# The entry of a two-layer transformer kernel: group 0's padded queries and keys from padded weights, later norms on ACT

## The chip, the cores and the metric

The kernel runs on one core of one Trainium2 chip. The metric is the device time of one execution in microseconds (us). The core has the matrix engine PE (its weight loads are listed apart as PEld), the vector engine DVE, the scalar engine ACT, GpSimd (POOL), and SyncE (SP), which here issues nearly all DMA transfers. The engines run apart from one another and meet at semaphores. Each takes its own instructions strictly in order, so an instruction that waits holds back everything behind it on its engine.

## The reference

Input is x, 4 sequences of 512 tokens of width 128 (2048 tokens). Four sublayers follow, each as `x = x + f(layernorm(x))`:

```
Q, K, V = heads(x @ WQ), heads(x @ WK), heads(x @ WV)      # 16 heads of width 8
score = Q K^T / sqrt(8) + causal mask; softmax; out = P V; out @ WO
mixture of 8 experts, top 2, capacity limit, GELU
gated linear recurrence (16 heads of 64) and an FFN, itself a pre-norm block
FFN of ternary weights: silu(xW1)*(xW2), two GELU layers, W3
```

Only the entry matters here: the first layernorm, `Q` and `K` of sequence 0, and the first score tiles of the first attention.

## The kernel before, in words

**Work units.** Attention goes by batch (sequence) b = 0..3 and by group g = 0..3 of four heads; w (or G) = 4b + g numbers the 16 groups. For each group PE computes ten row tiles of 128 queries by 4 heads x 128 keys (`row_scores`, fp32r, into one of three PSUM banks that rotate, `ROWB = 3`), and DVE takes the maximum of each (`row_max`). `minus_max` forms the negated maxima, PE turns them (`turn_max`), DVE adds them into the queries (`add_max`, QM), and then the second pass begins: `key_scores` on PE, exp on ACT, a causal select on POOL, `values` on PE. The row tiles of group w+1 run between the second-pass tiles of group w. A group takes about 10 us in steady state.

**Padded operands.** A head is only 8 wide. To keep fp32 accuracy in fp32r, Q and K are split into a rounded high part and a low rest, and each head takes 32 partitions: for the queries the planes high, low, high, 0; for the keys high, high, low, 1. The fourth plane later carries the maximum. In the kernel before, every group gets these padded tiles through DRAM: `project(b)` (two fp32 matmuls, L1537 and L1538) writes Q and K, ACT rounds them (`round_halves`, L659), DVE subtracts to get the low part (`make_halves`, L977), SP stores six planes into `qk_dram` (`store_planes`), and `pad(G)` reads back QS (queries, one DMA, L398) and KP (keys, four DMAs, one per head, block-diagonal over zeros that POOL has set, L407).

**The entry.** SP loads x by batch. DVE makes the statistics of batch 0 (L960 to L967), POOL the reciprocal root (a power, L494), DVE the norm (L947, `first_norm`). PE turns the normed tile (`first_turn`, L1516), ACT copies it out (`keep_x`, L645), PE projects. The statistics of batches 1 to 3 are one stretch of twelve tiles on DVE. Their norms come on DVE behind `make_halves(0)`. For each batch PE then does a turn and the values' projection (`first_v`, L1525), and ACT copies both out (`keep_x`, `keep_v`). Only when all four batches are done does PE start `row_scores(0, 0)`. Behind the ten tiles of group 0 stand a wait for the last `keep_v`, the first two row tiles of group 1, and `turn_max(0)`.

**What sets the order.** Nothing is scheduled by a planner: each engine's program is written out by hand in its order, and PSUM banks are handed over by counters (`rs_full`, `row_free`). `RING` numbers the uses of the three row banks: the Q and K projections of batch 0 take places 0 and 1 (banks 0 and 1), group 0's tiles the places from 2 on.

Of the kernel before, what the change touches and what calls it, by code (L numbers as in the profile page):

```python
# [13 lines left out]
P = 128  # L14
NB = 4
# [26 lines left out]
N_CONST = 3 * P + 16 + 2 * NT + 8  # L42
# [66 lines left out]
def build(nc, d):  # L109
    ctx = ExitStack()  # L110
    with ctx:
# [3 lines left out]
        def sem(name):  # L115
            return ctx.enter_context(nc.semaphore(name))
# [15 lines left out]
        iota8 = const[:, 3 * P + 16 + 2 * NT:3 * P + 24 + 2 * NT]  # L132

# [116 lines left out]

        ones = low["h2_w"][:, FF - 1, :].bitcast(F32)
# [34 lines left out]
        var0, rs0, xn0, tp0, tc0, vp0, vc0 = (sem(n) for n in ("var0", "rs0", "xn0", "tp0", "tc0", "vp0", "vc0"))  # L286
        l0 = sem("l0")
# [63 lines left out]
        def _(sp):  # L351
# [38 lines left out]
            def pad(G):  # L390

                b, g = G // NG, G % NG
                if g == 0:
                    sp.wait_ge(pads_out[b], 32)
                    sp.wait_ge(q_planes, 48 * (b + 1))
# [4 lines left out]
                if g == 0:  # L400
                    sp.wait_ge(k_planes, 48 * (b + 1))
# [8 lines left out]
            pad(0)  # L410
# [71 lines left out]
        def _(g):  # L482
# [12 lines left out]

            first_rsqrt(0, slice(0, TB))
            set_keys(0)
            first_rsqrt(1, slice(TB, NT))
            set_keys(1)
# [132 lines left out]
        def _(act):  # L632
# [262 lines left out]
        def _(v):  # L895
# [610 lines left out]
        def _(pe):  # L1506
            pe.wait_ge(par_in, 32)
# [145 lines left out]
            for u in range(10):
                row_scores(0, u)
# [385 lines left out]
def shape_constants():  # L2040
# [17 lines left out]
    c[:, at:at + 8] = np.arange(8)  # L2058

# [33 lines left out]
```

## Time and profile before

| | us |
|---|---|
| median of 3 runs | 664.29 (663.62 to 668.38) |
| profiled execution, its own time | 664.96 |
| its span | 663.2 |
| granted TensorE clock, mean over the span | 0.963 |
| PE busy | 579.7 (87%) |
| DVE busy | 406.9 (61%) |
| ACT busy | 308.9 (47%) |
| POOL busy | 172.6 (26%) |

A span runs from the first to the last profiled instruction; the execution's own time has 1.8 us more around it. Busy shares are averages over the whole program, and the change touches only its first few dozen microseconds, so what counts is the order of time there: which instruction is released by which.

### The profile page before, as it was taken

To read this page: it belongs to the slowest core of one execution; us is meant where nothing else is said; L and a number is where in the kernel's file an instruction comes from. 1 tells how busy PE (TensorE), PEld (TensorE's weight loads), DVE (VectorE), ACT (ScalarE), POOL (GpSimd) and SP (SyncE) were. 2 spreads that over 40 slices of the span, in tenths; PEclk is the share of its full clock that TensorE was granted. 3 is DMA by queue.
4 is the path that set the end of the run, shared out by engine and by line. 5 is a ranking of instruction groups with operands and counts; after the bars stand their busy time and mean duration, and the time that the engine had idled before them with its cause. 6 is when DMAs were issued, how large, how long until landed. Compare 5 with 4: busy or idle time off the path is not lost.

```text
span 663.2 us, 9219 instructions
## 1 busy us (share of the span) xinstructions
PE 579.7 (87%) x3331; PEld 433.6 (65%) x3331; DVE 406.9 (61%) x959; ACT 308.9 (47%) x527; POOL 172.6 (26%) x184
## 2 busy tenths in 40 slices
PE   2689999999999559999828698899999999998987
PEld 1546656556665346877726486688778878786866
DVE  5678868978886421332237985994569656762330
ACT  3336665555656213453305343852565355653351
POOL 4302212352452640000057643601400041001100
PEclk9999999999999759999959897999999999999999
DMA  4746241262210425753111000000000000000000
GB/s 133 220 128 217 96 138 35 64 192 64 72 57 1 123 77 194 236 177 113 32 51 27 22 16 1 25 9 1 0 17 1 0 1 17 1 0 1 16 1 17
DMA packets 45645, 43.02 MB, mean 65 GB/s; under 512 B 4256, under 2 KB 34976, under 8 KB 45600
## 3 DMA queue, kind: packets, MB, share of 16 engines
q1 hardware_dynamic: 43264, 37.96, 18.9%
q0 software_dynamic: 2048, 4.20, 2.1%
q8 instruction: 27, 0.44, 0.3%
q10 hardware_dynamic: 288, 0.27, 0.2%
q14 instruction: 18, 0.15, 0.1%
HBM read 25.64 MB, written 16.78 MB: 64 GB/s over the span
## 4 chain that ended last, share of the span: by engine, by line
PE 70%; DVE 11%; issue 7%; ACT 7%; DMA 2%; POOL 2%; SPq 1%; DVEq 0%; ACTq 0%; POOLq 0%
PE ps L1865 7%; PE ps L1818 6%; PE ps L1547 6%; PE ps L1809 5%; PE ps L1563 5%; PE ps L1575 5%; PE ps L1887 5%; PE ps L1888 4%; PE ps L1968 4%; PE ps L1964 4%; PE ps L1965 4%; PE ps L1891 4%; DVE pm L987 2%; PE ps L1881 2%; PE ps L1550 2%
## 5 line engine op out<-in xcount | busy, mean ns | idle before, releaser
L669 ACT ACTIVATE PT<-ps 128x384 f32<-128x384 f32 (+1 forms) x192 | 93.4, 529 | 75.2 <-PE ps L1563 69.6
L987 DVE TENSOR_REDUCE pm<-ps 128x4 f32<-128x512 f32 x160 | 102.0, 684 | 11.7 <-PE ps L1547 11.3
L1547 PE MATMUL ps<-KP,QS 128*128 128x512 f32 x160 | 72.2, 453 | 6.1 <-DVEq L980 3.2
L536 POOL TENSOR_SCALAR_AFFINE_SELECT PT<-PT 128x512 f32<-128x512 f32 x64 | 39.9, 636 | 133.9 <-ACT PT L669 133.1
L1563 PE MATMUL ps<-QM,KP 128*128 128x512 f32 (+3 forms) x256 | 69.2, 331 | 1.6 <-DVE QM L1001 1.1
L1563 PEld LDWEIGHTS ps<-QM,KP 128*128 128x128 f32 x256 | 43.7, 189 | 23.0 <-issue 13.4
L757 ACT ACTIVATE HT<-ps,cols 128x640 f32<-128x640 f32 x32 | 25.4, 793 | 54.9 <-PE ps L1809 54.9
L1547 PEld LDWEIGHTS ps<-KP,QS 128*128 128x128 f32 x160 | 29.9, 188 | 27.2 <-DVE pm L987 13.5
L1352 DVE TENSOR_TENSOR_SCAN zero<-decay,OG 128x512 f32<-128x512 f32 x32 | 44.8, 1401 | 1.1
L1575 PE MATMUL ps<-PT,V 128*32 128x128 f32 (+3 forms) x512 | 44.6, 442 | 0.0
L511 POOL TENSOR_TENSOR rstd<-veps,mhalf 128x4 f32<-128x4 f32 x11 | 12.7, 1157 | 111.4 <-DVE veps L924 111.2
L1818 PE MATMUL ps<-W,HT 128*128 128x128 f32 x320 | 37.9, 278 | 3.1 <-ACT HT L757 3.1
L1818 PEld LDWEIGHTS ps<-W,HT 128*128 128x128 f32 x320 | 36.3, 192 | 5.3 <-ACT HT L757 5.3
L1809 PE MATMUL ps<-XST,W 128*128 128x320 f32 x128 | 36.5, 438 | 1.1 <-DVE XST L1253 1.1
L814 ACT ACTIVATE hF<-ps,cols 128x512 f32<-128x512 f32 x16 | 11.0, 687 | 56.1 <-PE ps L1968 56.1
L1347 DVE SCALAR_TENSOR_TENSOR OG<-ps,cols,vs 128x512 f32<-128x512 f32 x32 | 24.0, 749 | 18.1 <-ACT vs L793 14.2
L797 ACT ACTIVATE gs<-ps,half_bg 128x512 f32<-128x512 f32 x32 | 22.0, 688 | 26.7 <-PE ps L1891 25.6
L601 POOL DMA_INDIRECT G<-ys_dram,posG x8 | 7.6, 950 | 93.1 <-DMA ys_dram<-zero 91.0
L572 POOL DMA_INDIRECT G<-ys_dram,posG x24 | 29.3, 1221 | 6.8 <-issue 6.8
L793 ACT ACTIVATE vs<-ps,cols 128x512 f32<-128x512 f32 x32 | 22.0, 687 | 19.2 <-PE ps L1891 19.1
L1809 PEld LDWEIGHTS ps<-XST,W 128*128 128x128 f32 x128 | 22.4, 190 | 12.1 <-ACT HT L757 4.4
L1865 PEld LDWEIGHTS ps<-lwo,oT 128*128 128x128 f32 x256 | 29.1, 192 | 0.2
(279 smaller groups left out, 1303.1 us busy)
## 6 DMA issues: line engine op xcount, KB each, us to landing
qk_dram<-HL SPq DMA_DIRECT2D x24, 256.0 KB
QS<-qk_dram SPq DMA_DIRECT2D x16, 256.0 KB
KP<-qk_dram SPq DMA_DIRECT2D x64, 64.0 KB
W<-in_eW SPq DMA_DIRECT2D x16, 256.0 KB
xs_dram<-zero SPq DMA_DIRECT2D x4, 640.0 KB, 3.7
XS<-xs_dram SPq DMA_DIRECT2D x8, 320.0 KB, 4.6
ys_dram<-zero SPq DMA_DIRECT2D x8, 320.0 KB, 2.9
whole_h_w<-in_h_w SPq DMA_DIRECT2D x2, 1024.0 KB, 9.1
```

The lines of the kernel that those rows point to most:

```text
L536: g.affine_select(out=diag, in_=diag, pattern=[[0, 4], [1, P]], compare_op=ALU.is_ge, fill=0.0, base=0, channel_multiplier=-1).then_inc(se ...
L572: g.indirect_dma_start(out=G[:, b % 2, i, :], out_offset=None, in_=ys_dram, in_offset=bass.IndirectOffsetOnAxis(ap=posG[:, c:c + 1], axis= ...
L669: act.activation(PT[:, i, a:z], bank[ROWB + n % KEYB][:, 0:z - a], ACT.Exp, scale=float(DK) ** -0.5).then_inc(exp_done, 1)
L987: v.tensor_reduce(pm[:, t, k, :], bank[n % ROWB].rearrange("p (i n) -> p i n", n=P), AXX, ALU.max).then_inc(row_free[n % ROWB], 1)
L1352: v.tensor_tensor_scan(st, decay[:, f:f + 1].to_broadcast([P, SEQ]), kv, 0.0, ALU.mult, ALU.add).then_inc(st_done, 1)
L1547: mm = pe.matmul(to, QS[:, G % 2, t * P:(t + 1) * P], KP[:, G % 3, k, :, :].rearrange("p i n -> p (i n)"), start=True, stop=t != k)
L1563: mm = pe.matmul(bank[ROWB + n % KEYB][:, at:at + SEQ - j * P], KP[:, w % 3, j, i, :], QM[:, w % 2, j * P:SEQ], start=True, stop=True)
L1575: mm = pe.matmul(bank[6][32 * i:32 * i + 32, j * P:SEQ], V[:, j * H + g * 4 + i, :], PT[:, i, OFF[j]:OFF[j + 1]], start=(j == 0), stop=(j ...
L1809: mm = pe.matmul(ps[:, 2 * (f % 2) + a, 0:HALF], W1[:, s, f * P:(f + 1) * P], XST[:, s, a * HALF:(a + 1) * HALF], start=True, stop=True)
L1818: mm = pe.matmul(bank[4 + j // 4][:, (j % 4) * P:(j % 4 + 1) * P], HT[:, s, f, j * P:(j + 1) * P], W2[:, s, f, :], start=(f == 0), stop=(f ...
L1865: mm = pe.matmul(bank[5][:, t * P:(t + 1) * P], src[:, f, t * P:(t + 1) * P], w[:, f, :], start=(f == 0 and t == 0), stop=(f == n - 1), sk ...
L1887: pe.matmul(to, high[n][:, cs], halves_of[:, 0, :], start=True, stop=False)
```

## The change

Group 0's padded tiles are no longer read back from DRAM. DVE clears two 128x128 tiles (in a part of VR that is not in use yet) and copies columns of WK and WQ into them, four heads at 32 columns each, with the sign of the plane (for the keys w, w, -w, 0; for the queries w, -w, w, 0). Two fp32 matmuls with these weights (into banks 3 and 7) give the padded keys and queries at once. ACT writes the rounded value, and one DVE instruction adds or subtracts the exact value with a per-partition factor 0 or -1 (three new columns of `const`), so that each plane becomes its high or low part. The padded queries land in QS directly. The keys are spread into their diagonal blocks by two DVE and two ACT copies of 32 partitions. Groups 1 to 3 of batch 0 still come through DRAM, so the plain projections, the halves and the stores stay; `pad(1)` is now the first load.

The norms of batches 1 to 3 move from DVE to ACT, as x * rstd + (-mean * rstd). DVE makes -mean, POOL the product. POOL's two first clears of KP move ahead of its first power, DVE's clears of MX and pm move to its very start. PE gets six matmuls on a tile of zeros before anything else, and the ten row tiles of group 0 stand between the turns and value projections of batches 1 to 3. `ROWB` stays 3.

PE, from its start to the first `turn_max` (L1516 first_turn, L1525 first_v, L1547 and L1550 row_scores and its mask, L1589 turn_max), before:

```order
L1516 MATMUL ps<-const,xn 128x128 x4
L1537 MATMUL ps<-xnT,wq 128x512
L1538 MATMUL ps<-xnT,wk 128x512
L1516 MATMUL ps<-const,O 128x128 x4
L1525 MATMUL ps<-wv,xnT 128x128 x4
L1516 MATMUL ps<-const,xn 128x128 x4
L1525 MATMUL ps<-wv,xnT 128x128 x4
L1516 MATMUL ps<-const,O 128x128 x4
L1525 MATMUL ps<-wv,xnT 128x128 x8
L1547 MATMUL ps<-KP,QS 128x512 x2
```

And the same place in the changed kernel (L1711 and L1713 are the padded keys and queries, L1581 first_turn, L1590 first_v, L1615 and L1618 row_scores):

```order
L1571 MATMUL ps<-zero 128x512 x6
L1581 MATMUL ps<-const,xn 128x128 x4
L1711 MATMUL ps<-xnT,VR 128x512
L1713 MATMUL ps<-xnT,VR 128x512
L1602 MATMUL ps<-xnT,wq 128x512
L1603 MATMUL ps<-xnT,wk 128x512
L1590 MATMUL ps<-wv,xnT 128x128 x4
L1615 MATMUL ps<-KP,QS 128x512 x2
L1618 MATMUL ps<-mask,identr 128x512
L1615 MATMUL ps<-KP,QS 128x512 x2
L1581 MATMUL ps<-const,O 128x128 x4
L1615 MATMUL ps<-KP,QS 128x512
```

The row tiles now start behind batch 0's value projection, and batch 1's turn stands behind four of them; the two padded projections stand ahead of the plain ones.

ACT, from batch 0's turned tile (L655 keep_x) to its last copy of values (L659 keep_v) in the changed kernel (L715 and L717 round the padded tiles, L709 spreads keys, L669 rounds the plain halves, L704 is the norm):

```order
L655 ACTIVATE xnT<-ps 128x512
L715 ACTIVATE low_Wv<-ps,const 128x512
L717 ACTIVATE QS<-ps 128x512
L709 ACTIVATE KP<-low_Wv 32x4x128 x2
L669 ACTIVATE HL<-ps 128x512 x2
L659 ACTIVATE VR<-ps 128x512
L704 ACTIVATE O<-X,VR,rstd 128x128 x4
L655 ACTIVATE xnT<-ps 128x512
L704 ACTIVATE xn<-X,VR,rstd 128x128 x4
L659 ACTIVATE VR<-ps 128x512
L655 ACTIVATE xnT<-ps 128x512
L704 ACTIVATE O<-X,VR,rstd 128x128 x4
```

Before, ACT had only the L645, L649 and L659 copies here; the twelve norm instructions are new, and so are the four on padded tiles, which stand ahead of the halves that the stores wait for.

POOL, its first instructions in the changed kernel (L492 clears KP, L502 the powers, L509 the product, L510 clears V):

```order
L496 MEMSET low_h_w 128x512
L492 MEMSET KP 128x2048 x2
L502 ISA
L502 TENSOR_TENSOR rstd<-veps,mhalf 128x4
L502 TENSOR_TENSOR rstd<-veps,mhalf 128x12
L509 TENSOR_TENSOR VR<-VR,rstd 128x12
L510 MEMSET V 128x2048
```

Before, the row marked ISA (a setting that POOL takes ahead of its first power) stood right behind the clear of low_h_w, and each power had a clear of KP behind it.

The diff, with comments and the parts that only repeat left out:

```diff
@@ -132 +133 @@
+low_q, low_k, pad_k = (const[:, N_CONST - 3 + i:N_CONST - 2 + i] for i in range(3))
@@ -250 +252 @@
+wqp = VR[:, NT - 1, :]
+wkp = VR[:, NT - 2, :]
+first_k = low["Wv"][:, 0:SEQ]
+nm0 = VR[:, NT - 3, 0:NT]
+nmr0 = VR[:, NT - 3, NT:2 * NT]
@@ -393 +402 @@
-        if g == 0:
+        if g == 0 or G == 1:
@@ -400 +409 @@
-        if g == 0:
+        if g == 0 or G == 1:
@@ -410 +418 @@
-    pad(0)
@@ -496 +503 @@
-    first_rsqrt(0, slice(0, TB))
@@ -498 +504 @@
-    first_rsqrt(1, slice(TB, NT))
@@ -499 +506 @@
+    first_rsqrt(0, slice(0, TB))
+    first_rsqrt(1, slice(TB, NT))
+    g.wait_ge(rs0, 2)
+    g.tensor_tensor(nmr0[:, TB:NT], nm0[:, TB:NT], rstd0[:, TB:NT], ALU.mult).then_inc(rs0, 1)
@@ -688 +699 @@
+    def first_norm(b):
+        dst = (xn, O)[b % 2]
+        if b >= 2:
+            act.wait_ge(tp0, b - 1)
+        for t in range(b * TB, (b + 1) * TB):
+            ins = act.activation(dst[:, t % TB, :], X[:, t, :], ACT.Identity, scale=rstd0[:, t:t + 1],
+                                 bias=nmr0[:, t:t + 1])
+        ins.then_inc(xn0, 1)
+    def spread_keys(i):
+        act.activation(KP[32 * i:32 * i + 32, 0, :, i, :],
+                       first_k[32 * i:32 * i + 32, :].bitcast(F32).rearrange("p (t n) -> p t n", n=P),
+                       ACT.Copy).then_inc(first_a_set, 1)
@@ -689 +714 @@
+    act.wait_ge(first_full, 1)
+    act.activation(first_k, bank[3], ACT.Identity, bias=pad_k).then_inc(first_high, 1)
+    act.wait_ge(first_full, 2)
+    act.activation(QS[:, 0, :], bank[7], ACT.Identity).then_inc(first_high, 1)
+    act.wait_ge(first_sum, 1)
+    act.wait_ge(kp_set, 1)
+    spread_keys(2)
+    spread_keys(3)
@@ -691 +723 @@
-    for b in range(1, NB):
-        keep_x(b)
-        keep_v(b - 1)
-    keep_v(NB - 1)
+    keep_v(0)
+    act.wait_ge(rs0, 3)
+    first_norm(1)
+    keep_x(1)
+    first_norm(2)
+    keep_v(1)
+    keep_x(2)
+    first_norm(3)
+    keep_v(2)
+    keep_x(3)
+    keep_v(3)
@@ -940 +979 @@
-    def first_norm(b):
-        dst = (xn, O)[b % 2]
-        v.wait_ge(rs0, min(b, 1) + 1)
-        if b >= 2:
+    v.memset(wqp, 0.0).then_inc(wp_zero, 1)
+    v.memset(wkp, 0.0).then_inc(wp_zero, 1)
+    v.memset(MX[:, :, :, :].bitcast(F32), 0.0)
+    v.memset(pm[:, :, :, :], -3.0e38)
@@ -945 +984 @@
-            v.wait_ge(tp0, b - 1)
-        for t in range(b * TB, (b + 1) * TB):
-            ins = v.tensor_scalar(dst[:, t % TB, :], X[:, t, :], mv0[:, t, 0:1], rstd0[:, t:t + 1],
-                                  ALU.subtract, ALU.mult)
-        ins.then_inc(xn0, 1)
-    for ts in (range(0, TB), range(TB, NT)):
-        if ts[0]:
-            first_norm(0)
-            v.memset(MX[:, :, :, :].bitcast(F32), 0.0)
-            v.memset(pm[:, :, :, :], -3.0e38)
+    def first_stats(ts):
@@ -966 +996 @@
+        if ts[0]:
+            v.tensor_scalar(nm0[:, c], mv0[:, c, 0], -1.0, None, ALU.mult)
@@ -968 +1000 @@
+    def planes(w):
+        return w.rearrange("p (h c r) -> p h c r", h=4, c=4)
+    def of_heads(w, n):
+        return w[:, 0:4 * DK].rearrange("p (h a r) -> p h a r", h=4, a=1).to_broadcast([P, 4, n, DK])
+    first_stats(range(0, TB))
+    v.wait_ge(wqk_in, 32)
+    v.wait_ge(wp_zero, 2)
+    v.tensor_copy(planes(wkp)[:, :, 0:2, :], of_heads(wk, 2))
+    v.tensor_scalar(planes(wkp)[:, :, 2:3, :], of_heads(wk, 1), -1.0, None, ALU.mult).then_inc(wp_set, 1)
+    v.tensor_copy(planes(wqp)[:, :, 0:3:2, :], of_heads(wq, 2))
+    v.tensor_scalar(planes(wqp)[:, :, 1:2, :], of_heads(wq, 1), -1.0, None, ALU.mult).then_inc(wp_set, 1)
+    v.wait_ge(rs0, 1)
+    for t in range(TB):
+        ins = v.tensor_scalar(xn[:, t, :], X[:, t, :], mv0[:, t, 0:1], rstd0[:, t:t + 1], ALU.subtract, ALU.mult)
+    ins.then_inc(xn0, 1)
+    first_stats(range(TB, NT))
+    def add_low(n, dst, src, sign, done):
+        v.wait_ge(par_in, 32)
+        v.wait_ge(first_high, n)
+        v.scalar_tensor_tensor(out=dst, in0=src, scalar=sign, in1=dst.bitcast(F32), op0=ALU.mult,
+                               op1=ALU.add).then_inc(done, 1)
+    add_low(1, first_k, bank[3], low_k, first_sum)
+    v.wait_ge(first_sum, 1)
+    v.wait_ge(kp_set, 1)
+    for i in (0, 1):
+        v.tensor_copy(KP[32 * i:32 * i + 32, 0, :, i, :],
+                      first_k[32 * i:32 * i + 32, :].bitcast(F32).rearrange("p (t n) -> p t n", n=P)
+                      ).then_inc(first_v_set, 1)
+    add_low(2, QS[:, 0, :], bank[7], low_q, first_v_set)
@@ -1090 +1154 @@
-    first_norm(1)
-    first_norm(2)
-    first_norm(3)
@@ -1506 +1569 @@
+    pe.wait_ge(zero_set, 1)
+    for _ in range(6):
+        pe.matmul(bank[7], zero[:, 0:P], zero[:, 0:SEQ], start=True, stop=True)
@@ -1543 +1608 @@
-        if u == 0:
-            pe.wait_ge(qs_in[G % 2], 16 * (G // 2 + 1))
-            pe.wait_ge(kp_in[G % 3], 64 * (G // 3 + 1))
+        if u == 0 and G == 0:
+            pe.wait_ge(first_v_set, 3)
+            pe.wait_ge(first_a_set, 2)
+        elif u == 0:
+            pe.wait_ge(qs_in[G % 2], 16 * ((G + 1) // 2))
+            pe.wait_ge(kp_in[G % 3], 64 * ((G + 2) // 3))
@@ -1641 +1710 @@
+    pe.wait_ge(wp_set, 1)
+    pe.matmul(bank[3], wkp, xnT[:, 0:SEQ], start=True, stop=True).then_inc(first_full, 1)
+    pe.wait_ge(wp_set, 2)
+    pe.matmul(bank[7], wqp, xnT[:, 0:SEQ], start=True, stop=True).then_inc(first_full, 1)
@@ -1644 +1715 @@
-    first_turn(1)
@@ -1647 +1718 @@
-    first_turn(2)
+    pe.wait_ge(bfc, 4)
+    row_scores(0, 0)
+    row_scores(0, 1)
+    row_scores(0, 2)
+    row_scores(0, 3)
+    first_turn(1)
+    row_scores(0, 4)
+    row_scores(0, 5)
@@ -1649 +1727 @@
-    first_turn(3)
+    first_turn(2)
+    row_scores(0, 6)
+    row_scores(0, 7)
@@ -1650 +1731 @@
+    first_turn(3)
+    row_scores(0, 8)
+    row_scores(0, 9)
@@ -1652 +1734 @@
-    pe.wait_ge(bfc, 4)
-    for u in range(10):
-        row_scores(0, u)
@@ -2058 +2139 @@
+    at += 8
+    plane = i % 32 // 8
+    c[:, at] = np.where(plane == 1, -1.0, 0.0)
+    c[:, at + 1] = np.where(plane == 2, -1.0, 0.0)
+    c[:, at + 2] = plane == 3
```

## Rows read from the trace of the kernel before

**Rows 1.** The chain in order of time, 0 to 110 us: start, length, what.

```profile
17.77 4.68 DVE O L947 x3
22.49 1.11 PE ps L1516 x4
...
30.14 6.08 DVE pm L987 x10
...
37.79 0.69 DVE QM L1001
```

**Rows 2.** Timeline, DVE, 4 to 49 us: start, length, line, instruction, xcount, idle before.

```profile
7.93 2.37 DVE L947 TENSOR_SCALAR xn<-X,mv,rstd 128x128 f32<-128x128 f32 x4 [1.20 <-POOL rstd L494]
...
10.84 2.35 DVE L960 BATCH_NORM_STATS2 stats<-X 128x6 f32<-128x128 f32 x12
...
14.27 0.17 DVE L967 TENSOR_SCALAR veps<-mv 128x12 f32<-128x12 f32 x1
...
17.51 4.93 DVE L947 TENSOR_SCALAR O<-X,mv,rstd 128x128 f32<-128x128 f32 x4 [0.15 <-DVE HL L977]
22.36 1.10 DVE L947 TENSOR_SCALAR xn<-X,mv,rstd 128x128 f32<-128x128 f32 x4
```

**Rows 3.** Timeline, PE, 10 to 50 us.

```profile
10.45 1.08 PE L1516 MATMUL ps<-const,xn 128*128 128x128 f32 x4 [10.45 <-DVE xn L947]
...
14.09 1.91 PE L1538 MATMUL ps<-xnT,wk 128*128 128x512 f32 x2
...
27.37 0.60 PE L1516 MATMUL ps<-const,O 128*128 128x128 f32 x4
...
42.72 1.12 PE L1537 MATMUL ps<-xnT,wq 128*128 128x512 f32 x2
...
46.26 0.45 PE L1547 MATMUL ps<-KP,QS 128*128 128x512 f32 x1
...
48.31 0.50 PE L1547 MATMUL ps<-KP,QS 128*128 128x512 f32 x1 [1.21 <-DVEq L980]
```

**Rows 4.** Timeline, ACT, 4 to 31 us.

```profile
5.30 0.31 ACT L636 ACTIVATE identr<-const 128x128 fp32r<-128x128 f32 x1 [2.22 <-DMA cols<-in_cols]
...
30.40 0.62 ACT L696 ACTIVATE V<-VR 128x512 f32<-128x512 f32 x1
```

**Rows 5.** Timeline, POOL, 0 to 40 us.

```profile
1.93 0.53 POOL L488 MEMSET low_h_w<- 128x512 f32 x1
6.88 1.01 POOL L494 TENSOR_TENSOR rstd<-veps,mhalf 128x4 f32<-128x4 f32 x1 [4.42 <-DVE veps L967]
7.84 1.81 POOL L484 MEMSET KP<- 128x2048 f32 x1
14.53 2.28 POOL L494 TENSOR_TENSOR rstd<-veps,mhalf 128x12 f32<-128x12 f32 x1 [4.88 <-DVE veps L967]
```

**Rows 6.** Timeline, SP's queue, 14 to 49 us.

```profile
14.95 1.16 SPq L381 DMA_DIRECT2D qk_dram<-HL  x2
...
22.39 2.52 SPq L407 DMA_DIRECT2D KP<-qk_dram  x4
...
28.10 0.60 SPq L373 DMA_DIRECT2D qk_dram<-zero  x1
...
33.83 0.44 SPq L415 DMA_DIRECT2D rows<-in_w_s  x1
...
38.88 2.50 SPq L407 DMA_DIRECT2D KP<-qk_dram  x4
```

**Rows 7.** Answer on DMA issues: size each, median us from issue to landing at the end.

```profile
X<-in_x SPq DMA_DIRECT2D x4, 256.0 KB, 4.6
...
out_dram<-zero SPq DMA_DIRECT2D x4, 256.0 KB, 2.3
```

**Rows 8.** Timeline, DVE and then POOL, 340 to 352 us.

```profile
349.38 0.60 DVE L1328 TENSOR_SCALAR O<-X,mv,rstd 128x128 f32<-128x128 f32 x2 [0.33 <-POOL rstd L607]
...
349.32 1.00 POOL L608 TENSOR_TENSOR rstd<-veps,mhalf 128x4 f32<-128x4 f32 x1
```

More of the change, by code:

```diff
@@ L41 @@
 OFF = [sum(SEQ - i * P for i in range(j)) for j in range(TB + 1)]
-N_CONST = 3 * P + 16 + 2 * NT + 8
+N_CONST = 3 * P + 16 + 2 * NT + 8 + 3
 COLS = [("ln1_g", 1), ("ln1_b", 1), ("ln2_g", 1), ("ln2_b", 1), ("bq", LF), ("bk", LF), ("bv", LF), ("bg", LF),
@@ L286, in build @@
         var0, rs0, xn0, tp0, tc0, vp0, vc0 = (sem(n) for n in ("var0", "rs0", "xn0", "tp0", "tc0", "vp0", "vc0"))
+        wp_zero, wp_set = sem("wp_zero"), sem("wp_set")
+        first_full, first_high, first_sum = sem("first_full"), sem("first_high"), sem("first_sum")
+        first_v_set, first_a_set = sem("first_v_set"), sem("first_a_set")
         l0 = sem("l0")
@@ L494, in first_rsqrt @@
                 g.tensor_tensor(rstd0[:, c], veps0[:, c], mhalf[:, c], ALU.pow).then_inc(rs0, 1)
+            set_keys(0)
+            set_keys(1)
             first_rsqrt(0, slice(0, TB))
-            set_keys(0)
             first_rsqrt(1, slice(TB, NT))
-            set_keys(1)
+            g.wait_ge(rs0, 2)
+            g.tensor_tensor(nmr0[:, TB:NT], nm0[:, TB:NT], rstd0[:, TB:NT], ALU.mult).then_inc(rs0, 1)
             g.memset(V[:, :, :], 0.0).then_inc(setup, 1)
@@ L1641, in _ @@
             pe.wait_ge(tc0, 1)
+            pe.wait_ge(wp_set, 1)
+            pe.matmul(bank[3], wkp, xnT[:, 0:SEQ], start=True, stop=True).then_inc(first_full, 1)
+            pe.wait_ge(wp_set, 2)
+            pe.matmul(bank[7], wqp, xnT[:, 0:SEQ], start=True, stop=True).then_inc(first_full, 1)
             pe.wait_ge(wqk_in, 32)
             project(0)
-            first_turn(1)
             pe.wait_ge(w0_in, 48)
             first_v(0)
+            pe.wait_ge(bfc, 4)
[6 more added lines that the diff above has]
+            row_scores(0, 5)
+            first_v(1)
             first_turn(2)
-            first_v(1)
+            row_scores(0, 6)
+            row_scores(0, 7)
+            first_v(2)
             first_turn(3)
-            first_v(2)
+            row_scores(0, 8)
+            row_scores(0, 9)
             first_v(3)
-            pe.wait_ge(bfc, 4)
-            for u in range(10):
-                row_scores(0, u)
             pe.wait_ge(vc0, NB)
```

## The prediction

> **What bounds the kernel now.** The chain in order of time comes first, since the change touches only the entry. From 17.77 us it runs through three DVE norms of batch 1 (4.68 us), then PE's turns and value projections from 22.49, then ten row maxima (30.14, 6.08 us), and at 37.79 DVE adds the first maxima into the queries [rows 1]. I call that instruction QM; the second pass of group 0 hangs on it. Behind it nothing waits for the entry any more, so the question is how much earlier QM comes. Next DVE's timeline: the four norms of batch 1 take 4.93 us where the same four of batch 2 take 1.10, and batch 0's took 2.37 [rows 2]; POOL's clear of KP, 1.81 us from 7.84, lies over the latter [rows 5]. Then PE: it stands idle after the plain projections (14.09, 1.91 us) [rows 3] until 22.49. Last SP's queue: the planes' stores begin at 14.95, the loads of KP for group 0 at 22.39, those of group 1 are through when the next stores begin at 28.10 [rows 6]. So group 0 waits for batches 1 to 3, which wait for slow norms; its own DRAM trip ends only a little sooner.
>
> **The path up to the first row tile.** POOL is idle for 4.42 us before its first power; two clears of 1.8 us behind 2.46 end at 6.1, so the power still starts at 6.88 and ends at 7.89 [rows 5]. DVE's four small copies of weights stand in its 1.20 us idle stretch before the norm; at about 0.17 us each they fit [rows 2]. Cost nothing; without that cover, up to 0.7. The norm now has no clear beside it: 1.10 instead of 2.37, ending at 9.05.
>
> PE's six matmuls start at about 2.0, when POOL's zero tile is set, since its next clear starts at 1.93 [rows 5]. A projection takes 1.91 us at PE's slow pace (1.2 GHz) and 1.12 at the fast one (2.4), there with the next start 0.96 later. From 22.49 PE worked 4.9 us before four transposes fell to 0.60 us from 1.08 [rows 1, 3]. With 4.9 us at the slow pace and the rest fast, the six end at 10.2; all fast 8, all slow 13.4. So batch 0's turn runs from 10.2 to 10.8 instead of 10.45 to 11.53, and the copy of 512 columns (0.62) [rows 4] ends at 11.45. Padded keys then end at 12.6 and padded queries at 13.5; the plain projections, which stood first before, end at 14.4 and 15.4, and the value projection of batch 0 (eight passes, twice a turn's work) near 16.2.
>
> ACT rounds the keys to 13.25 and the queries to 14.15. DVE's statistics of twelve tiles took from 10.84 to 14.44, 3.6 us [rows 2]; from 9.05, with one more small row, they end at 12.75. DVE corrects the keys (0.69, as QM [rows 1]) to 14.0. The spread is two copies each on DVE and ACT. ACT's 512-wide copy from on-chip memory is 0.62 [rows 4]. DVE's is in no row: between half of QM's 0.69 and all of it; I take 0.55. Both end at 15.2. Queries are corrected to 15.9; row tile 0 can run from 16.2. DVE makes the plain low halves first (to 17.4), so row maxima run from 17.45, and ten at 0.6 would end at 23.5.
>
> **The path behind it.** Batches 1 to 3 now hang on ACT. A 128x128 instruction of ACT is 0.31 [rows 4]; a norm has a scale and a bias column besides, which no row of this shape has. Ends: 0.31, and 0.62, what four times the columns cost. I take four norms at 1.3 us. POOL's long power ends at 12.75 + 2.28 = 15.1 [rows 5], its product near 15.5; ACT comes to it later, at 16.9, behind the spreads, two roundings and a copy of values. Per batch ACT then has 1.3 of norms and two copies of 0.6, with 0.5 for PE's turn between: batch 1 is normed at 18.2, batch 2 at 21.0, batch 3 at 23.5. PE's last two row tiles stand behind batch 3's turn, so the last maximum ends at 25.8, and the last copy of values at 26.9. PE waits for it before group 1's first tile.
>
> Group 1 comes through DRAM. The first store needs ACT's rounded queries, 15.8 instead of 14.95. Stores and their landing took 22.39 - 14.95 = 7.44 us, which gives 23.25; the four loads are issued to 25.8 (2.52 before) [rows 6]. Landing of KP is in no row: for 256 KB the shortest median is 2.3 and x takes 4.6 [rows 7]. I take 2.3 after the start of the last, as these are 64 KB each: 27.5. It ends last, by 0.6. The tile, the second one and the turn of maxima follow, and QM comes at 29.1. **It was 37.79: 8.7 us less.**
>
> **Is it given back?** SP issues six pad stores and three loads between group 1 and group 2, 28.10 to 34.27, 6.17 us [rows 6]. They now end at 32.0, so group 2's KP is issued to 34.9 (2.50 us) and lands at 36.6 to 38.9. PE wants it at 46.26 - 8.7 = 37.6. It may be 1.3 late, but PE then stands 1.21 us before 48.31 for another reason [rows 3], which takes this up. I charge nothing. Everything later is released by instructions, so it moves as a whole.
>
> The profiled execution took 664.96: 664.96 - 8.7 = 656.3. The median is 0.67 lower, which gives 655.6. **I take 656.0.**
>
> **A rule weighed.** A norm of DVE that ran from 349.38 beside POOL's power at 349.32 kept its 0.60 for two, while a clear slowed norms to 4.93 us for four [rows 2, 8]. I therefore let DVE's spread copies run beside the long power (12.8 to 15.1), which is the sum above. The Trainium skill, "SBUF — State Buffer", on the engines' ports, says that DVE (in its two-port modes) and GpSimd take a shared port pair as an exclusive lock for a whole instruction. By that rule the copies would wait for the power, and then perhaps for the clear of V; rows 8 speak against the first half and rows 2 for the second.
>
> **Rivals.**
> 1. *POOL holds DVE's spread copies* (chance 0.18). The power ends at 15.1, the clear of V lies from 15.5 to about 17.3. One copy at 15.1 and the other behind the clear: queries corrected at 18.4, halves at 19.9, row maxima 2.3 us later and all of ACT's chain with them. 658.2; with only the first wait, 657.2. For it: [rows 2]; against: [rows 8], and that the copies are finished at 15.2 only if DVE is on time, with 0.3 us to spare.
> 2. *Group 1's load is the bound and is slow* (0.12). Landing after 4.6 instead of 2.3: QM at 31.4, 658.3. For it: the loads were issued until 28.10 before, and move by only 2.3 us. Against: DMA has no other work just then.
> 3. *POOL's setting ahead of the power costs time* (0.05). Its row in the order now stands behind the clears; the 4.42 us that hid it are down to 0.8. Price 0 to 3.6: up to 659.6.
> 4. *PE stays slow on a tile of zeros* (0.03). No row shows PE's pace rising on zeros. The six end at 13.4, turn and two padded projections are slow: 5.4 us later, 661.4. That is the change not doing one thing that it is built to do.
> 5. *Slower than before* (0.02). ACT's norms are the one place. PE takes batch 1's turn in order, and six row tiles, group 1 and QM stand behind the three batches. QM would be back at 37.8 if the twelve norms took 8.7 us more, 1.0 us each instead of 0.31; slower by 1% needs 1.6 each. For it: a pair of column operands on ACT at this shape is nowhere in the trace. Against: 512 columns take 0.62. At 1.8 us each it would be 674.
>
> **Chances and range.** The forecast as worked out has 0.60, with its own range 653.9 to 657.8: the low end has a DVE copy at 0.35, a turn as soon as batch 0 is normed (1.1 us), and 0.3 of landing; the high end norms of 0.45 each. Cases 1 to 3 reach to 659.6. The runs before spread from 663.62 to 668.38 for one kernel, so a median can stand a little off as well. Range 652.9 to 660.2, with some 0.08 left out above it (cases 4 and 5 and what I have not seen) and 0.1 below. This kernel's measurement tells about 1% from no change, 6.6 us here, so faster means under 657.6: 0.57 from the forecast, 0.07 from case 1, 0.03 from case 2. Faster 0.67, within 1% 0.30, slower 0.03.
>
> **What would show it.** PE's turn of batch 0 near 10.2 and 0.60 long; DVE's norm of batch 0 near 1.1; the first row tile near 16.2; four norms of ACT in 1.3; QM near 29.1, and PE's wait before group 1's first tile ended by the DMA of KP, not by ACT. Wrong would be: DVE copies of 32 partitions far over 0.7 us (case 1), a gap of POOL before 7.89 (case 3), transposes of 1.08 at 10 us (case 4), or QM early and group 2's first tile later than 38.9, which would be the queue of SP giving it back.

## The result, and the profile after

| | before | changed |
|---|---|---|
| median | 664.29 us (663.62 to 668.38, 4 runs) | 656.33 us (656.27 to 657.69, 4 runs) |
| ratio | | 0.9879, 95% interval 0.9848 to 0.9910 |
| profiled execution, its span | 664.96, 663.2 | 656.35, 654.6 |
| mean granted TensorE clock | 0.963 | 0.965 |
| QM, first of 16 | 37.79 | 29.05 |
| QM, second and sixteenth | 49.78, 210.09 | 41.24, 201.88 |

The changed kernel is 1.2% faster. Sum and forecast were 656.3 and 656.0 us, and QM was put at 29.1. The span is 8.6 us shorter, of which 8.74 came in ahead of QM. Behind it 0.5 was handed back by the sixteenth QM, and the rest of the kernel took 452.7 us against 453.1. That the rest took the same is no rule: in two more traces of the changed kernel it took 455.7 and 455.3 (next section).

DVE's timeline of the changed kernel comes first, as in [rows 2]. L1015 is batch 0's norm, L1022 the correction of the padded keys and queries, L1029 the spread copies, L1052 the row maxima, L1066 QM.

```profile
7.72 1.11 DVE L1015 TENSOR_SCALAR xn<-X,mv,rstd 128x128 f32<-128x128 f32 x4 [0.72 <-POOL rstd L502]
...
13.25 0.75 DVE L1022 SCALAR_TENSOR_TENSOR low_Wv<-ps,const,low_Wv 128x512 fp32r<-128x512 f32 x1 [0.76 <-ACT low_Wv L715]
14.03 0.86 DVE L1029 CAST KP<-low_Wv 32x512 fp32r<-32x512 f32 x2
...
17.63 3.68 DVE L1052 TENSOR_REDUCE pm<-ps 128x4 f32<-128x512 f32 x6
...
25.34 1.29 DVE L1052 TENSOR_REDUCE pm<-ps 128x4 f32<-128x512 f32 x2 [1.59 <-PE ps L1615]
...
29.05 0.69 DVE L1066 TENSOR_TENSOR QM<-QS,ps 128x512 fp32r<-128x512 f32 x1 [0.21 <-PE ps L1657]
```

The norm (L1015) has no clear beside it and takes 1.11 us where [rows 2] have 2.37. Nothing here takes 4.93 any more. PE's timeline shows what the three batches cost now.

```profile
2.05 8.11 PE L1571 MATMUL ps<-zero 128*128 128x512 f32 x12 [2.05 <-POOL zero L495]
10.00 0.60 PE L1581 MATMUL ps<-const,xn 128*128 128x128 f32 x4
11.29 1.12 PE L1711 MATMUL ps<-xnT,VR 128*128 128x512 f32 x2 [0.69 <-ACT xnT L655]
...
15.78 0.47 PE L1615 MATMUL ps<-KP,QS 128*128 128x512 f32 x1
...
27.61 0.73 PE L1615 MATMUL ps<-KP,QS 128*128 128x512 f32 x2 [0.69 <-ACT VR L659]
...
39.60 0.47 PE L1615 MATMUL ps<-KP,QS 128*128 128x512 f32 x1 [1.92 <-DMA KP<-qk_dram]
```

The turn of batch 0 is at 10.00 and fast (0.60 against 1.08 in [rows 3]). At 27.61 stands group 1's first tile, released by ACT's last copy of values (L659, 26.96 to 27.56), and at 39.60 group 2's first tile, which waits 1.92 us for its load. ACT's and then POOL's timeline:

```profile
14.03 1.27 ACT L709 ACTIVATE KP<-low_Wv 32x512 fp32r<-32x512 f32 x2
...
16.93 1.65 ACT L704 ACTIVATE O<-X,VR,rstd 128x128 f32<-128x128 f32 x4
19.36 0.60 ACT L655 ACTIVATE xnT<-ps 128x512 f32<-128x512 f32 x1 [0.78 <-PE ps L1581]
19.86 1.64 ACT L704 ACTIVATE xn<-X,VR,rstd 128x128 f32<-128x128 f32 x4
...
26.96 0.60 ACT L659 ACTIVATE VR<-ps 128x512 f32<-128x512 f32 x1 [1.25 <-PE ps L1590]
```

```profile
6.67 1.01 POOL L502 TENSOR_TENSOR rstd<-veps,mhalf 128x4 f32<-128x4 f32 x1 [0.72 <-DVE veps L998]
12.57 2.38 POOL L502 TENSOR_TENSOR rstd<-veps,mhalf 128x12 f32<-128x12 f32 x1 [4.89 <-DVE veps L998]
```

SP's queue, as in [rows 6]: the stores begin at 15.96, group 1's loads at 23.29, group 2's at 33.02. One pad store took 1.80 us, where the others take 0.60.

```profile
15.96 1.16 SPq L390 DMA_DIRECT2D qk_dram<-HL  x2
...
23.29 2.51 SPq L416 DMA_DIRECT2D KP<-qk_dram  x4
...
29.07 1.80 SPq L384 DMA_DIRECT2D qk_dram<-low_h_w  x1
...
33.02 2.48 SPq L416 DMA_DIRECT2D KP<-qk_dram  x4
```

The landing of group 1's four loads is on record in this trace. The view of line L416 from 23 to 26 us gives 2.2 to 2.3 us for each:

```profile
L416 SPq DMA_DIRECT2D KP<-qk_dram x4: 588/592/599, 23.3 to 25.2; - x4
DMA to landing us min/median/max: 2.2/2.2/2.3
```

The last was issued at 25.20 and landed at 27.43, so it was 0.13 us ahead of ACT's copy.

### The profile page after: what moved, and what is told of

Read it like the earlier page. It is cut to its first block, busy times and chain, and to the rows that moved or that the text cites. A ratio compares the mean times of both kernels' runs of the same rounds, so it can differ in the third digit from the quotient of the medians.

```text
span 654.6 us, 9264 instructions
## 1 busy us (share of the span) xinstructions
PE 583.0 (89%) x3347; PEld 433.0 (66%) x3347; DVE 402.2 (61%) x958; ACT 316.2 (48%) x543; POOL 172.9 (26%) x185
## 4 chain that ended last, share of the span: by engine, by line
PE 66%; DVE 10%; ACT 7%; issue 6%; DMA 5%; POOL 4%; SPq 2%; DVEq 0%; POOLq 0%; ACTq 0%
PE ps L1945 7%; PE ps L1615 6%; PE ps L1898 5%; PE ps L1631 5%; PE ps L1643 5%; PE ps L1967 5%; PE ps L1968 4%; PE ps L1889 4%; PE ps L2048 4%; PE ps L2044 4%; PE ps L2045 4%; PE ps L1971 4%; PE ps L1961 2%; DMA XS<-xs_dram 2%; PE ps L1618 2%
## 5 line engine op out<-in xcount | busy, mean ns | idle before, releaser
L1052 DVE TENSOR_REDUCE pm<-ps 128x4 f32<-128x512 f32 x160 | 102.3, 681 | 10.0 <-PE ps L1615 9.4
L1615 PE MATMUL ps<-KP,QS 128*128 128x512 f32 x160 | 71.7, 452 | 7.9 <-DVEq L1045 2.5
L1631 PEld LDWEIGHTS ps<-QM,KP 128*128 128x128 f32 x256 | 43.8, 189 | 22.8 <-issue 12.6
L1615 PEld LDWEIGHTS ps<-KP,QS 128*128 128x128 f32 x160 | 29.8, 188 | 27.5 <-DVE pm L1052 11.5
L1945 PEld LDWEIGHTS ps<-lwo,oT 128*128 128x128 f32 x256 | 29.1, 192 | 0.2
```

The lines of the kernel that those rows point to most:

```text
L1052: v.tensor_reduce(pm[:, t, k, :], bank[n % ROWB].rearrange("p (i n) -> p i n", n=P), AXX, ALU.max).then_inc(row_free[n % ROWB], 1)
L1615: mm = pe.matmul(to, QS[:, G % 2, t * P:(t + 1) * P], KP[:, G % 3, k, :, :].rearrange("p i n -> p (i n)"), start=True, stop=t != k)
L1631: mm = pe.matmul(bank[ROWB + n % KEYB][:, at:at + SEQ - j * P], KP[:, w % 3, j, i, :], QM[:, w % 2, j * P:SEQ], start=True, stop=True)
L1945: mm = pe.matmul(bank[5][:, t * P:(t + 1) * P], src[:, f, t * P:(t + 1) * P], w[:, f, :], start=(f == 0 and t == 0), stop=(f == n - 1), sk ...
```

## The experiments

A kernel's time also holds what happens hundreds of microseconds behind the entry (last part of this section), so each entry is judged by when its QMs come. QM times are us from the span's start, and "QM 16 to the end" is a length in us. Each row's times come from one trace. The medians were taken in four sittings, on several chips, and the ratio is to the kernel before in the same sitting.

| kernel | QM 1 | QM 2 | QM 3 | QM 16 | QM 16 to the end | median | ratio, interval |
|---|---|---|---|---|---|---|---|
| before | 37.79 | 49.78 | 59.49 | 210.09 | 453.1 | | |
| clears alone | 35.09 | 47.09 | 56.82 | 207.45 | 456.7 | 661.59 | 0.9928 (0.9898 to 0.9957) |
| group 0 from DRAM | 34.15 | 46.15 | 55.88 | 207.30 | 457.7 | 662.72 | 0.9962 (0.9935 to 0.9988) |
| norms on DVE | 31.95 | 43.95 | 53.67 | 204.09 | 454.1 | 659.27 | 0.9914 (0.9888 to 0.9940) |
| no zero matmuls | 29.96 | 41.95 | 51.68 | 202.40 | 454.5 | 658.19 | 0.9911 (0.9886 to 0.9936) |
| clears back | 29.52 | 41.51 | 51.49 | 202.19 | 452.9 | 659.04 | 0.9925 (0.9899 to 0.9951) |
| pads late | 29.15 | 41.16 | 52.44 | 203.10 | 455.0 | 659.69 | 0.9893 (0.9835 to 0.9951) |
| changed | 29.05 | 41.24 | 51.24 | 201.88 | 452.7 | 656.33 | 0.9879 (0.9848 to 0.9910) |
| changed, second time | 28.32 | 40.32 | 50.07 | 200.73 | 455.7 | 658.07 | 0.9867 (0.9817 to 0.9916) |
| changed, third time | 28.35 | 40.34 | 50.13 | 200.78 | 455.3 | 656.58 | 0.9855 (0.9820 to 0.9891) |
| improved | 27.27 | 39.26 | 48.98 | 199.36 | 456.7 | 657.85 | 0.9861 (0.9808 to 0.9914) |
| improved, second time | 27.62 | 39.62 | 49.33 | 199.73 | 453.8 | 655.70 | 0.9854 (0.9816 to 0.9892) |
| improved, pads early | 27.16 | 39.16 | 48.98 | 199.39 | 453.3 | 656.24 | 0.9871 (0.9824 to 0.9918) |

**Group 0 from DRAM.** The kernel before with the clears first, the six matmuls and the norms on ACT. Group 0 still comes back from DRAM and the row tiles stand behind all four batches. Two places of the diff:

```diff
+    for _ in range(6):
+        pe.matmul(bank[7], zero[:, 0:P], zero[:, 0:SEQ], start=True, stop=True)
@@ ACT
     round_halves(0)
+    act.wait_ge(rs0, 3)
+    first_norm(1)
+    keep_x(1)
+    first_norm(2)
...
```

> Only the new way of group 0 is undone: it comes back through DRAM, and its ten row tiles stand behind all four batches again; the norms on ACT, the six matmuls on zeros and POOL's clears ahead of the power stay. Theory 1 (the on-chip tiles carry a good half of the gain, as the entry is one path to QM): stores start near 13.1, all batches are through near 24.7, first row tile there, QM 8.2 later at 32.9, 3.9 later than in the changed kernel, of which 0.5 is hidden by group 2's load: 659.7 us. Theory 2 (the cheap parts carry it, since group 1 still needs the DRAM trip): QM at most 1 us later, 657.

QM came at 34.15, past the first theory's 32.9 by 1.25, and the median at 662.72, past its 659.7 by 3.0, of which the long way behind QM 16 (457.7) holds a part. The second theory, at most 1 us later, falls. PE's timeline, and then all engines' busy time from 15 to 22 us; PE's granted clock is the figure behind the fifth count, 0.54:

```profile
17.04 1.12 PE L1538 MATMUL ps<-const,O 128*128 128x128 f32 x4 [4.59 <-ACT O L698]
17.95 1.92 PE L1547 MATMUL ps<-wv,xnT 128*128 128x128 f32 x8
```

```profile
15.00:22.00 7.00, 4.45 (x20) 4.16 (x21) 0.00 (x0) 4.73 (x11) 4.13 (x8) 0.54 0.70 219
```

PE stood idle 4.59 us, and the clock fell to the 1.2 GHz level: batch 1's turn took 1.12 us (0.60 in the changed kernel) and the values 1.92 (1.05). Without group 0's row tiles between them, the batches leave PE empty. So the tiles on the chip and their place in PE's order are together worth 34.15 - 29.05 = 5.1 of the 8.7 us, and the three smaller edits 3.6. No run parts the tiles from their place. Against the changed kernel's other two traces the 5.1 would be 5.8.

**Clears alone.** The kernel before with POOL's two clears of KP ahead of its first power.

```diff
+    set_keys(0)
+    set_keys(1)
     first_rsqrt(0, slice(0, TB))
-    set_keys(0)
     first_rsqrt(1, slice(TB, NT))
-    set_keys(1)
```

> The kernel before with one part of the change alone: POOL's two first clears of KP ahead of its powers. Theory 1 (DVE's norms ran into the clears): batch 0's norm takes 1.1 instead of 2.4 us, batch 1's norm meets one clear less and ends near 19.5 instead of 22.4; QM comes 2 to 3 us earlier, 661.5 to 662.5. Rival (group 0's DRAM trip is nearly as late as the turns, so at most 1.3 comes through): 663.2.

QM came 2.70 us earlier, inside what was expected. DVE:

```profile
7.82 1.11 DVE L947 TENSOR_SCALAR xn<-X,mv,rstd 128x128 f32<-128x128 f32 x4 [1.13 <-POOL rstd L494]
...
16.14 3.18 DVE L947 TENSOR_SCALAR O<-X,mv,rstd 128x128 f32<-128x128 f32 x4 [0.15 <-DVE HL L977]
```

Batch 0's norm has its 1.11. Batch 1's falls from 4.93 to 3.18 us. It still meets two clears, that of V and that of the third part of KP, where it met three before (KP, V, KP). POOL:

```profile
15.38 1.80 POOL L500 MEMSET V<- 128x2048 f32 x1
...
17.33 1.85 POOL L484 MEMSET KP<- 128x2048 f32 x1
```

**Clears back** (a clear again between the powers, in the changed kernel, and the other behind them).

```diff
-    set_keys(0)
-    set_keys(1)
     first_rsqrt(0, slice(0, TB))
+    set_keys(0)
     first_rsqrt(1, slice(TB, NT))
...
+    set_keys(1)
```

> The changed kernel with POOL's clears of KP behind the powers again, one between them and one behind the product. Theory 1: batch 0's norm on DVE takes 2.4 instead of 1.1 us and ends near 10.1, but PE's six matmuls end at 10.0 and hide it; the statistics end 1.3 later, so the keys are corrected 0.6 later and QM comes 0.2 to 0.7 later: 656.5 to 657.0. Rival (the clears are worth what they take off the norm): 657.6.

QM moved by 0.47, and the profiled execution took 656.86, as the main theory had it. The median, 659.04 (656.84 to 660.84), is above what either gave, and nothing at the entry explains it. DVE's norm of batch 0 has its 2.37 back:

```profile
7.78 2.37 DVE L1015 TENSOR_SCALAR xn<-X,mv,rstd 128x128 f32<-128x128 f32 x4 [0.82 <-POOL rstd L502]
```

PE was busy with zeros until 10.36 there, so most of the 1.26 us lay beside them. Alone the clears were worth 2.70, as the last piece 0.47 (0.27 once the end of the zeros is allowed for, see "second and third time" below).

**No zero matmuls.**

```diff
-    pe.wait_ge(zero_set, 1)
-    for _ in range(6):
-        pe.matmul(bank[7], zero[:, 0:P], zero[:, 0:SEQ], start=True, stop=True)
```

> The changed kernel without the six matmuls on zeros. Theory 1: the turn starts at 8.85 instead of 10.0 but at the slow pace, padded keys end near 12.6, and PE gets fast only near 15.5; ACT's first norm starts 1.6 us later than 16.9, QM at 30.1 to 30.7: 657.4 to 658. If PE stays slow to the value projection, 659.5. Rival (the six matmuls only hold PE back): the turn is 1.1 us earlier and the time falls to 655.5.

QM came at 29.96: 0.9 later than in the changed kernel's first trace and 1.6 later than in the other two, in which the six ended at 9.43 and 9.39 and not at 10.16. PE:

```profile
9.10 1.09 PE L1578 MATMUL ps<-const,xn 128*128 128x128 f32 x4 [9.10 <-DVE xn L1015]
10.87 2.07 PE L1708 MATMUL ps<-xnT,VR 128*128 128x512 f32 x2 [0.69 <-ACT xnT L655]
12.73 1.54 PE L1710 MATMUL ps<-xnT,VR 128*128 128x512 f32 x2
```

The turn starts 0.9 us sooner, since no zeros stand in its way, and then turn and both padded projections run slow. The zeros pay for themselves, but only by the difference of the two. The first theory (30.1 to 30.7) held within 0.2 us, and the rival, that they only hold PE back, falls.

**Norms on DVE.** The twelve norms go back to DVE, one batch at a time between the row maxima.

```diff
+    late_norm(1)
+    row_max(0, 0)
+    row_max(0, 1)
+    late_norm(2)
...
@@ ACT
-    act.wait_ge(rs0, 3)
-    first_norm(1)
```

> The changed kernel with the norms of batches 1 to 3 on DVE again, placed behind the halves and between the row maxima; ACT keeps only its copies. Theory 1 (ACT's chain of norms and copies sets QM by a hair): batch 1's norm meets POOL's clears of V and KP until 19.0 and ends at 19.3, the others take 1.1 each between the maxima, and QM comes at 29.0 to 29.6: 656 to 657. Rival (moving the norms to ACT is what pays): DVE's row of maxima ends 3.3 us later and the clears slow each norm, 659 to 660.

The rival was right in time: QM 31.95, 659.27 us. DVE, POOL, PE:

```profile
16.56 2.43 DVE L1152 TENSOR_SCALAR O<-X,mv,rstd 128x128 f32<-128x128 f32 x4
...
20.11 1.10 DVE L1152 TENSOR_SCALAR xn<-X,mv,rstd 128x128 f32<-128x128 f32 x4
```

```profile
12.33 2.28 POOL L502 TENSOR_TENSOR rstd<-veps,mhalf 128x12 f32<-128x12 f32 x1 [4.82 <-DVE veps L990]
14.56 1.81 POOL L508 MEMSET V<- 128x2048 f32 x1
...
16.51 1.83 POOL L492 MEMSET KP<- 128x2048 f32 x1
```

```profile
19.64 0.79 PE L1624 MATMUL ps<-KP,QS 128*128 128x512 f32 x1 [2.62 <-DVE pm L1044]
...
22.88 1.91 PE L1599 MATMUL ps<-wv,xnT 128*128 128x128 f32 x8
```

Batch 1's norm ran into the clear at 16.51, cost 1.33 us extra and ended at 18.99, as I had expected (19.3). What I had left out is what stood behind it: the row maxima kept PE's banks, PE stood 2.62 us, and its granted clock was 0.56 from 18 to 24 us, with 1.91 for a value projection. Here the entry itself was early, since the zeros ended at 8.95 and the first row tile ran at 14.70 and not at 15.78, so this trace gives the price, 2.9 us, no closer than by 1 us. Without the two accidents the norms may be no worse on DVE than on ACT; no run shows that. The improved kernel below keeps one batch there, behind the clears.

**Pads late.** Six pad stores and three broadcast rows move in SP's queue from ahead of group 2's load to behind it.

```diff
-    for b in range(1, NB):
-        store_pads(b)
     for G in range(2, NW):
         pad(G)
+        if G == 2:
+            for b in range(1, NB):
+                store_pads(b)
```

> The changed kernel with one move in SP's queue: the six pad stores of batches 1 to 3 and the three loads of rows are issued behind group 2's load instead of ahead of it. QM stays at 29.05. Theory 1 (group 2's load, which landed at 39.5 behind them, gives back what it can, 0.5 us): the load is issued at 30 and lands near 34, PE's tile (2,0) runs at 37.7, the second one then waits for DVE's halves at 39.5 instead of 40.1, and the second QM comes 0.5 earlier, 655.8 us. Rival (the 1.9 us of PE's wait is all lost): 654.4.

Neither was right. The second QM came 12.01 us behind the first, as close as in the kernel before (11.99), but the third 11.28 behind the second (9.71 before). SP, then PE:

```profile
32.75 0.60 SPq L382 DMA_DIRECT2D qk_dram<-zero  x1
...
39.56 1.61 SPq L390 DMA_DIRECT2D qk_dram<-HL  x2
...
45.69 2.51 SPq L416 DMA_DIRECT2D KP<-qk_dram  x4
```

```profile
37.63 0.44 PE L1616 MATMUL ps<-KP,QS 128*128 128x512 f32 x1
...
39.68 0.50 PE L1616 MATMUL ps<-KP,QS 128*128 128x512 f32 x1 [1.21 <-DVEq L1046]
...
50.80 0.47 PE L1616 MATMUL ps<-KP,QS 128*128 128x512 f32 x1 [1.58 <-DMA KP<-qk_dram]
```

Group 2's first tile no longer waits for its load, but the next one then waits 1.21 us for DVE, as in [rows 3]. So the load's lateness was nearly hidden. The nine transfers now stood ahead of batch 1's stores and group 3's load, which was issued at 45.69 and not at 43.71, and PE waited there. Each place in the queue has someone behind it.

**Changed, second and third time.**

> The changed kernel itself once more, on the chip of the others: QM at 29.0, 656.3 us, the measure for the other three.

> The changed kernel once more, as the ruler for the two beside it. QM came at 29.05 and 28.32 us in its two traces so far, its medians were 656.3 and 658.1. Expected: QM 28.3 to 29.1, 657.2.

QM came at 28.32 and 28.35, since the clock rose sooner under the zeros, and the medians at 658.07 and 656.58. So 0.7 us of any comparison of QMs can come from this alone. Most of it can be taken out, because here QM follows the end of the zeros:

| kernel | zeros end | QM behind that |
|---|---|---|
| changed, three traces | 10.16, 9.43, 9.39 | 18.89, 18.89, 18.96 |
| clears back | 10.36 | 19.16 |
| pads late | 10.28 | 18.88 |
| improved, and a second time | 9.59, 10.01 | 17.67, 17.61 |
| improved, pads early | 9.45 | 17.71 |

The ruler doesn't serve for the two kernels in which something else holds the entry back, norms on DVE and group 0 from DRAM.

In the third trace group 2's first tile waited 1.51 us for its load, and still the second QM came 11.99 behind the first:

```profile
38.49 0.47 PE L1615 MATMUL ps<-KP,QS 128*128 128x512 f32 x1 [1.51 <-DMA KP<-qk_dram]
```

**Improved.** ACT rounds the plain halves ahead of and between its spread copies, so that the stores start sooner; batch 2's norm goes to DVE behind four row maxima; PE's wait for the last copy of values moves behind the first two tiles of group 1; the pads are dealt out behind the loads of groups 2, 3, 6 and 7.

```diff
+    round_first(0)
     spread_keys(2)
+    round_first(1)
     spread_keys(3)
-    round_halves(0)
@@ DVE
+    for n in range(4):
+        row_max(0, n)
+    for t in range(2 * TB, 3 * TB):
+        ins = v.tensor_scalar(xn[:, t % TB, :], X[:, t, :], mv0[:, t, 0:1], rstd0[:, t:t + 1],
@@ PE
-    pe.wait_ge(vc0, NB)
     row_scores(1, 0)
     row_scores(1, 1)
+    pe.wait_ge(vc0, NB)
```

> The changed kernel with four more moves: ACT rounds the plain queries and keys ahead of and between its two spreads, so that the stores start earlier; DVE makes the norm of batch 2 between its maxima; PE waits for the last copy of values only behind group 1's first two tiles; and the pad stores and rows stand behind the loads of groups 2, 3, 6 and 7. Theory 1 (QM hangs on ACT's chain and on group 1's load, both of which shorten): stores start at 14.8 and KP lands at 25.9, QM at 27.0, group 2's load is no longer late, and the second QM comes 2.0 to 2.5 us earlier: 654 us. Rival (PE falls to the slow pace again with the new gaps): QM at 29 or later, 656.

> The version with the pads moved and the lead of 1 us at QM, once more beside the changed kernel. Theory 1: its lead over the changed kernel, 1.1 to 1.4 us at the second, third and sixteenth QM, stands at the end, and the ratio to the kernel before is 0.002 lower than the changed kernel's. Theory 2: it is swallowed behind attention by the falls of PE's granted clock, which come at other times in each version, and the two read the same.

Then the same with the pads left where they were:

> The changed kernel with ACT's first rounding ahead of its spread copies and the second between them, batch 2's norm on DVE, and PE's wait for the last copy of values behind two tiles of group 1; the pads and broadcast rows stay in SP's queue ahead of group 2's load. Theory: QM comes at 27.2 to 27.6 as in the version with the pads moved, but group 2's load is issued behind the nine small transfers and lands near 36.8 to 38, so that the first tile of group 2 runs at 36.8 to 38.0 and not at 35.74, and some of the lead is lost there; at group 3 nothing is lost. End 0.8 below the changed kernel. Rival: the queue of SP does not bind here, and the fifth QM comes where it came with the pads moved.

QM came at 27.27, near the 27.0 expected, but the changed kernel that ran beside it stood at 28.32 and not at 29.05. The gain at the first QM is 1.05, and 0.73 the second time (27.62 against 28.35); at the sixteenth it is 1.37 and 1.05. With the pads early it is 1.19 and 1.39. Counted from the end of the zeros the lead at the first QM is 1.2 to 1.3 in all three traces. The 654 us that I expected were not reached, nor the lead of 2.0 to 2.5 us at the second QM: it is 1.06 against the trace beside it. So the load of group 2 doesn't bind, as the last rival said: with the pads early its tile waits 1.57 us at 37.37, and still the second QM (39.16 against 39.26) and the fifth (68.98 in both) come where they came with the pads moved.

```profile
37.37 0.47 PE L1631 MATMUL ps<-KP,QS 128*128 128x512 f32 x1 [1.57 <-DMA KP<-qk_dram]
```

In time the gain can't be told: 657.85 against 658.07, 655.70 and 656.24 against 656.58, with ratios whose intervals lie over one another. None of these versions is shown to beat the changed kernel.

**Where such a lead goes.** From the sixteenth QM to the end the kernels took 452.7 to 457.7 us, with the same instructions there (the changed kernel alone 452.7 to 455.7). Sixteen matmuls of the first expert are one place. The chain of waits of the changed kernel, and of the improved one:

```profile
241.87 4.66 PE ps L1889 x16
```

```profile
239.47 7.45 PE ps L1906 x16
```

And the engines' busy time over 7 us there, in the same order, with PE's granted clock behind the fifth count (1.00 and 0.53):

```profile
240.00:247.00 7.00, 5.90 (x26) 3.94 (x26) 0.89 (x2) 2.83 (x4) 0.00 (x0) 1.00 0.97 337
```

```profile
238.00:245.00 7.00, 5.91 (x15) 3.71 (x14) 0.89 (x2) 1.59 (x2) 0.00 (x0) 0.53 0.91 333
```

The improved kernel was 2.40 us ahead when they began and 0.39 behind when they ended, because the clock stood at 0.53 and not at 1.00. All thirteen traces fall into three sets by this stage, and the rest of the kernel goes with them: where it took 4.66 us (the kernel before, the changed one, clears back, improved with pads early) the way from QM 16 to the end was 452.7 to 453.3, where it took 6.1 to 6.4 (six traces) 453.8 to 455.7, and where it took 7.45 to 7.55 (clears alone, group 0 from DRAM, improved) 456.7 to 457.7. Before it PE works little, among POOL's scatters: in the changed kernel 18.78 of the 32.87 us from 201.88, at a mean clock of 0.71. What decides among the three is open: I made no run that only shifts the start of that stage.

## Why the prediction was right, step by step

**Up to the first row tile: right.** The six matmuls ended at 10.16 (10.2), the padded keys at 12.41 (12.6). The correction of the keys took 0.75 (0.69 taken), a DVE spread copy 0.43 (0.55 taken), and the row tile ran at 15.78 (16.2). The weight copies ended before POOL's power did and cost nothing. POOL's idle time ahead of its first power fell from 4.42 to 0.72 us without delaying it: 6.67 against 6.88 in [rows 5]. Rival 3 falls. That the six matmuls ended where the sum had them is in part luck: in the other two traces they ended at 9.43 and 9.39, and QM came 0.7 us sooner.

**The rule weighed: rival 1 falls, but a clear does hold DVE's norms.** The two CASTs ran from 14.03 to 14.89, inside POOL's power (12.57 to 14.95), at 0.43 each. By the rule of the Trainium skill, "SBUF — State Buffer", on the engines' ports, they would have waited until 14.95, if they count as DVE's two-port work, which no view shows. Against a clear the traces agree with that page of the Trainium skill: 2.43 us for four norms beside a MEMSET, 1.10 without, and 4.93 in [rows 2]; in the run with norms on DVE the clear ended at 18.33 and the norm that it held at 18.41. DVE's TENSOR_TENSOR on HL (15.96, 1.53 us for two, and 1.53 at 38.76 too) ran beside the clear of V and lost nothing. Of such an instruction, with one input in PSUM and only one in SBUF, the same page of the Trainium skill expects no waiting, and the trace agrees.

**ACT's norms: a term mis-sized.** Four took 1.65 and 1.64 us where the sum has 1.3. ACT began them at 16.93, as forecast (16.9). Three batches stand in a row, so the last copy of values ended at 27.56, where 26.9 was forecast.

**The releaser of group 1's first tile: wrong.** I had the DMA end last, at 27.5, by 0.6. The tile ran at 27.61 behind ACT's last copy, which ended at 27.56. The last of the four loads was issued at 25.20 and landed at 27.43, after 2.23 us; in the improved kernel with the pads early it took 2.4 (23.24 to 25.62). The median landing of all loads of KP, which the trace of before did not have, is in the answer on DMA issues (2.3 was taken):

```profile
KP<-qk_dram SPq DMA_DIRECT2D x60, 64.0 KB, 2.4
```

So the load was costed right within 0.1 us, and ACT's copy 0.66 too early; by luck it ended where the load had been put. The total was right, and this step of it was not.

**The path behind it: right in the sum, wrong in a bound.** Group 2's load was to be issued by 34.9 and to land at 36.6 to 38.9. It was issued by 35.50, since a pad store took 1.80, and had landed by about 39.5, where PE's wait ended, 4.6 us from the start of its last issue. The charge of nothing held nearly: PE waits 1.92 there, and the second QM lost 0.2 (12.19 behind the first, not 11.99). The next tile waits for DVE anyway, as [rows 3] showed with 1.21 us. The repeat shows where the bound is: there PE's wait ended 10.1 us behind the first QM and cost nothing, here 10.6 behind it, and cost 0.2. By the sixteenth QM 0.5 of the lead is gone; the other 0.3 I traced to the third QM and no further.

**"Everything later moves as a whole": not borne out.** It held in the trace that was forecast, 452.7 us against 453.1 behind the sixteenth QM. In the other two traces of the changed kernel the same stretch took 455.7 and 455.3. That sum and median met within 0.4 us is in part luck; the medians of the repeats, 658.07 and 656.58, lie in the forecast's range all the same.

**Zeros raise the pace: shown**, rival 4 falls: transposes of 0.60 at 10 us, and 1.09 without them. **Rival 2** falls, since the load of group 1 landed in 2.2 us. **Rival 5** was nowhere near: the norms took 0.41 each, and 1.0 was its point.

The share of each part in the 8.7 us depends on the order in which they are put in. The clears are 2.7 as the first edit and 0.5 or less as the last; the zeros and ACT's norms on top of the clears 0.9 together, and as the last edits 0.9 to 1.6 and about 3. The on-chip group with its row tiles between the batches is the largest part as the last edit, 5.1. It alone takes group 0 away from the end of all four batches. As the first edit I did not run it.

## What to carry to other kernels

An operand that is made by a trip through DRAM only to change its layout can often be made by a second matmul with rearranged weights; its worth is then less the trip than the work that may start before other inputs are ready. In a queue or on an engine that is filled in a fixed order, a transfer moved out of one's way is moved into somebody's: look who stands behind its new place. And judge a small edit at the entry by the first instruction that the rest hangs on, not by the end alone: here the remainder, with the same instructions, took 452.7 to 457.7 us.

## What the runs showed of the hardware

- Four of ACT's 128x128 instructions with a scale and a bias column, one behind the other, took 1.64 to 1.65 us; four of DVE's norms of that size took 1.10 to 1.11.
- A clear by POOL held DVE's norms (2.37 to 4.93 us for four, 1.10 without). A power by POOL held neither norms (power of 1.00 us, two norms in 0.60 [rows 8]) nor casts (power of 2.38 us, two casts in 0.86).
- Matmuls on zeros raised PE's granted pace, with 6.9 to 8.3 us for the six over the traces. Idle stretches of 2.62 and 4.59 us at the entry were followed by the slow level again (granted clock 0.56 from 18 to 24 us, and 0.54 from 15 to 22).
- The last KP load of 64 KB for group 1 landed 2.2 us after its issue began. That for group 2 took up to 4.6, behind six pad stores of 256 KB and three row loads of 64 KB, the last of which landed at 37.75, 5.7 us after its issue.
